# Half tiles, moved normalisations and later expert loads in a language-model tower on one core

## What is computed

```
h = table[ids]                                     # gather
h = h + causal_linear_attention(ln(h))             # 16 heads, elu features, then a scaled layer norm
h = h + ln(h) @ CB.T * (SCB / 127) + bias
h = h + block(ln(h))                               # random-feature attention, norm, relu FF 256-1024-256, norm
x = ln(h)
logits = x @ router_w.T                            # 8 experts, the best one is taken
score  = sigmoid(max(logits));  e = argmax(logits)
moe    = (silu(x*score @ gate[e]) * (x*score @ up[e])) @ down[e]
shared = (silu(x @ sgate) * (x @ sup)) @ sdown
out    = h + moe + shared
```

## Time and profile before

| | us |
|---|---|
| runs, median of three | 697.4 (695.35 to 697.88) |
| the profiled run, its own time | 697.74 |
| its span, first to last instruction | 695.9 |
| dense stage, to the end of the last `send_home` | 541.0 |
| from there to the first expert matmul (547.0) | 6.0 |
| expert matmuls of 23 tiles and the last add | to 692.2 |
| last scatter and its landing | to 695.9 |

### The profile page before, as it was taken

One profiled execution on the slowest core, in us unless ns is written; L12 is line 12 of the kernel. 1 busy time (PEld: TensorE's weight loads), 2 busy tenths in 40 slices (PEclk: granted clock), 3 DMA queues, 4 the chain that ended last, 5 costly groups with the idle time before them and its releaser, 6 DMA issues.

```text
span 695.9 us, 15601 instructions
## 1 busy us (share of the span) xinstructions
PE 638.5 (92%) x5962; PEld 518.7 (75%) x5963; DVE 496.9 (71%) x1156; ACT 288.8 (41%) x696; POOL 256.4 (37%) x414
## 2 busy tenths in 40 slices
PE   5887799998999999999999999999938699999996
PEld 4666687886888888888888989989937365655654
DVE  3988999999999989899989988886515122223231
ACT  2345456546565454546545445553310122222121
POOL 5342335435335152332504323312200355454442
PEclk9998999999999999999999999999987899999999
DMA  7950000000000000000000000003372211011110
GB/s 262 414 223 1 9 9 10 1 17 9 9 17 2 24 2 16 2 16 15 5 16 2 16 17 3 17 16 108 26 186 67 79 40 55 28 42 61 58 52 13
DMA packets 17299, 34.22 MB, mean 49 GB/s; under 512 B 7617, under 2 KB 12240, under 8 KB 15952
## 3 DMA queue, kind: packets, MB, share of 16 engines
q1 hardware_dynamic: 11776, 18.59, 7.4%
q0 software_dynamic: 4592, 8.41, 4.1%
q10 hardware_dynamic: 864, 6.29, 3.9%
HBM read 28.74 MB, written 7.29 MB: 52 GB/s over the span
## 4 chain that ended last, share of the span: by engine, by line
PE 68%; DVE 17%; issue 6%; DMA 4%; ACT 3%; another core or an unknown queue 0%; SPq 0%; POOLq 0%; POOL 0%; DVEq 0%; ACTq 0%
PE ps L1086 63%; DMA home_rows<-send_home 3%; PE ps L1091 2%; DVE stats L710 2%; DVE S_sb L769 2%; DVE rdenTA L792 1%; PE ps L1246 1%; DVE H L726 1%; DVE rdenTB L903 1%; ACT qkA L686 1%; DVE qf L882 1%; DVE mv L711 1%; DMA yA<-x_rows,ids 1%; ACT yTB L676 1%; DVE qkA L755 1%
## 5 line engine op out<-in xcount | busy, mean ns | idle before, releaser
L1086 PE MATMUL ps<-yTC,we 128*128 128x128 f32 x1024 | 124.9, 278 | 0.0
L1086 PEld LDWEIGHTS ps<-yTC,we 128*128 128x128 f32 x1024 | 121.5, 195 | 1.2 <-issue 0.2
L368 POOL TENSOR_TENSOR var_eps<-mv,ln_eps 128x1 f32<-128x1 f32 x112 | 24.3, 217 | 256.8 <-DVE mv L711 255.0
L1086 PE MATMUL ps<-we,yTA 128*128 128x256 f32 (+1 forms) x288 | 97.9, 476 | 3.2 <-DVE S_sb L769 1.4
L1086 PEld LDWEIGHTS ps<-we,yTA 128*128 128x128 f32 x288 | 55.4, 201 | 27.5 <-issue 22.3
L1086 PE MATMUL ps<-we,yTB 128*128 128x256 f32 (+1 forms) x216 | 72.8, 468 | 0.0
L369 POOL TENSOR_TENSOR rstd<-var_eps,pow_half 128x1 f32<-128x1 f32 x112 | 65.6, 586 | 8.8
L1086 PE MATMUL ps<-we,ffT 128*128 128x256 f32 x256 | 60.8, 380 | 0.0
L1086 PEld LDWEIGHTS ps<-we,yTB 128*128 128x128 f32 x216 | 39.7, 190 | 23.4 <-issue 21.0
L1086 PEld LDWEIGHTS ps<-we,ffT 128*128 128x128 f32 x256 | 47.2, 190 | 7.4
L578 ACT ACTIVATE kf<-kf 128x1024 f32<-128x1024 f32 x16 | 16.9, 1059 | 73.4 <-DVE kf L891 73.4
(11 more groups left out here) (189 smaller groups left out, 1364.5 us busy)
## 6 DMA issues: line engine op xcount, KB each, us to landing
we<-w_experts SPq DMA_DIRECT2D x4, 1536.0 KB
we<-w_experts ACTq DMA_DIRECT2D x3, 1536.0 KB
we<-w_ff SPq DMA_DIRECT2D x2, 1024.0 KB
x_rows<-send_x SPq DMA_DIRECT2D x16, 128.0 KB, 1.7
home_rows<-send_home SPq DMA_DIRECT2D x16, 128.0 KB, 1.8
rows_sb<-rows SPq DMA_DIRECT2D x1, 1664.0 KB, 6.4
we<-w_experts ACTq DMA_DIRECT2D x3, 512.0 KB, 3.9
we<-w_qk SPq DMA_DIRECT2D x2, 512.0 KB
```

Of the source, the lines that this page charges most:

```text
L368: link(pool.tensor_tensor(var_eps[:, k:k + 1], mv[:, k, 1:2], ln_eps[:], ALU.add))
L1086: return pe.matmul(o, a, b, start=start, stop=stop)
```

## The change

1. **Normalisations.** Norms 0, 2, 3 and 6 leave VectorE. GpSimd makes rstd as before and then two more products: mean * rstd, and that times -1 (`centre_at`). ScalarE then writes `Identity(x * rstd + centre)`.
2. **Tiles.** The expert stage has 10 rounds of two tiles: 16 whole tiles (W) and 4 tiles (H) that are each two halves of 64 tokens, each half with an expert of its own. An expert's rest of up to 64 tokens takes a half. A half's weights are fetched into `half_w`, which lies over h and the scores buffer (`H_S`), by a register-addressed DMA of 1.5 MB: two for each H tile. TensorE runs a half as a matmul with 64 stationary columns into 64 output partitions, the two halves by turns. New tables (`half_tables`, 22 small VectorE instructions) follow the last step.
3. **Loads.** Experts 4 to 7 are loaded by SP, after the first gather was transposed, instead of by ScalarE in the dense stage's last units. TensorE waits per tile for a count of experts (`experts_ready`), which SP raises.
4. **Order.** PSUM banks are dealt out anew, the four lists of steps are written in another order, waits that go with shared banks are others, and the expert loops are unrolled.

The core of the diff:

```diff
-    SORTED_TILES = T + E - 1
+    WHOLE, HALVES = T, E
+    SHAPES = ["WW", "WW", "WW", "WH", "WW", "WH", "WW", "WH", "WW", "WH"]
-    IDS_FROM = [0, MOE_SLOTS, 2 * MOE_SLOTS, 6 * MOE_SLOTS, SORTED_TILES]
+    IDS_FROM = [0, MOE_SLOTS, 2 * MOE_SLOTS, 3 * MOE_SLOTS, 5 * MOE_SLOTS, 7 * MOE_SLOTS, TILES]
...
             def ids3(t):
                 if t == T - 1:
+                    sp.wait_ge(S["table_ready"], 3)
                     load_ids(3)
             run_steps([
-                (0, x_out), (8, ids2), (2, ids0), (5, ids1), (3, home_out), (8, ids3),
+                (3, home_out), (1, ids0), (6, ids1), (8, ids2), (0, x_out), (8, ids3),
             ])
+            for name, count in (("ffn0_psum", T), ("out1_psum", T), ("ff2_psum", 2 * T), ("gate_psum", T), ("up_psum", T),
+                                ("down_psum", T), ("xT_psum", MOE_SLOTS)):
+                sp.wait_ge(S[name], count)
+            load_late(RESIDENT)
+            load_late(RESIDENT + 1)
+            load_ids(4)
+            load_late(RESIDENT + 2)
+            load_late(RESIDENT + 3)
+            sp.wait_ge(S["tile_done"], T)
+            sp.wait_ge(S["table_ready"], 2)
+            load_halves(0)
+            load_ids(5)
+            sp.wait_ge(S["residents_loaded"], 16 * RESIDENT)
+            sp.sem_inc(S["experts_ready"], 1)
+            for e in range(RESIDENT, E):
+                sp.wait_ge(late_loaded[e], 16)
+                sp.sem_inc(S["experts_ready"], 1)
+            for m in range(1, HALVES // 2):
+                before_it = [j for j in range(TILES) if KIND[j] == "H"][m - 1]
+                sp.wait_ge(S["ey_psum"], before_it + 1)
+                load_halves(m)
...
+            def deviation_and_centre(k, t):
+                link(inverse_deviation(k, t))
+                link(pool.tensor_tensor(centre_at[:, k:k + 1], mv[:, k, 0:1], rstd[:, k:k + 1], ALU.mult))
+                pool.tensor_tensor(centre_at[:, k:k + 1], centre_at[:, k:k + 1], minus_one[:], ALU.mult
+                                   ).then_inc(S[f"centre{k}_ready"], 1)
...
-            def normalise(dst, src, k, t):
-                dve.wait_ge(S[f"rstd{k}_ready"], t + 1)
-                return dve.tensor_scalar(dst, src, mv[:, k, 0:1], rstd[:, k:k + 1], ALU.subtract, ALU.mult)
+            def normalise(dst, src, k, t):
+                act.wait_ge(S[f"centre{k}_ready"], t + 1)
+                return act.activation(dst, src, ACT.Identity, bias=centre_at[:, k:k + 1], scale=rstd[:, k:k + 1])
...
+            def by_halves(o, x, at, n, chunks):
+                for c in range(chunks):
+                    for h in range(2):
+                        ins = matmul(o[h * HALF:(h + 1) * HALF], x[:, c, h * HALF:(h + 1) * HALF],
+                                     half_w[h][:, at + c * n:at + c * n + n], c == 0, c == chunks - 1)
+                return ins
...
+                for s, j in tiles_of(i):
                     pe.wait_ge(S["xT_ready"], j + 1)
+                    if KIND[j] == "W":
+                        pe.wait_ge(S["experts_ready"], need[s] if i < ALL_BY else E - RESIDENT + 1)
```

More of the change, by code:

```diff
@@ L47, in bass_lm_tower @@
     EXPERT = w_experts.shape[2]
-    SORTED_TILES = T + E - 1
-    ROUNDS = -(-SORTED_TILES // MOE_SLOTS)
+    HALF = P // 2
+    WHOLE, HALVES = T, E
+    SHAPES = ["WW", "WW", "WW", "WH", "WW", "WH", "WW", "WH", "WW", "WH"]
+    ROUNDS = len(SHAPES)
+    TILES = MOE_SLOTS * ROUNDS
+    KIND = "".join(SHAPES)
+    NUMBER = [KIND[:j].count(KIND[j]) for j in range(TILES)]
     SPAN = T + 1
@@ L65, in bass_lm_tower @@
         we = sb("we", [P, E * EXPERT])
-        H = sb("H", [P, T, D])
+        H_S = sb("H_S", [P, 2 * EXPERT])
+        H = H_S[:, 0:T * D].rearrange("p (t d) -> p t d", t=T)
+        S_sb = H_S[:, T * D:2 * EXPERT].rearrange("p (b a n) -> p b a n", b=4, a=4)
+        half_w = [H_S[:, h * EXPERT:(h + 1) * EXPERT] for h in range(2)]
         send_x, send_home = sb("send_x", [P, D]), sb("send_home", [P, D])
         nowhere = sb("nowhere", [P, E * SPAN + 1], U32)
-        ids = sb("ids", [P, SORTED_TILES], U32)
+        ids = sb("ids", [P, TILES], U32)
         idx_sb = sb("idx_sb", [P, T], U32)
@@ L110, in bass_lm_tower @@
         full = columns(T)
-        number = columns(SORTED_TILES)
+        number = columns(T + E - 1)
         start_row = columns(E)
@@ L209, in bass_lm_tower @@
         gathered = [sem(f"gathered{t}") for t in range(GATHERS)]
+        late_loaded = {e: sem(f"late_loaded{e}") for e in range(RESIDENT, E)}
+        half_loaded = [sem(f"half_loaded{h}") for h in range(2)]
         x_loaded = [sem(f"x_loaded{s}") for s in range(MOE_SLOTS)]
@@ L257, in tiles_of @@
         def tiles_of(i):
-            of_round = [(s, i * MOE_SLOTS + s) for s in range(MOE_SLOTS)]
-            return [(s, j) for s, j in of_round if j < SORTED_TILES] if isinstance(i, int) else of_round
+            return [(s, i * MOE_SLOTS + s) for s in range(MOE_SLOTS)]
         block = ctx.enter_context(nc.Block())
@@ L475, in ids_for @@
             def ids_for(i):
-                for n in range(4):
+                for n in range(GROUPS):
                     if IDS_FROM[n] == i * MOE_SLOTS:
-                        pool.wait_ge(S[f"ids_loaded{n}"], 16 * (IDS_FROM[n + 1] - IDS_FROM[n]))
+                        pool.wait_ge(S[f"ids_loaded{n}"], 16 * sum(2 if kind == "H" else 1 for kind in KIND[IDS_FROM[n]:IDS_FROM[n + 1]]))
             pool.drain()
@@ L626, in c_th @@
                 act.activation(tC[:], ga, ACT.Tanh, scale=0.5).then_inc(S["tanh_gate"], 1)
-            def load_experts(first, last, done):
-                for e in range(first, last):
-                    act.dma_start(we[:, e * EXPERT:(e + 1) * EXPERT], w_experts[e]).then_inc(S[done], 16)
-            def free_b(t):
-                if t == T - 1:
-                    act.wait_ge(S["ffn0_psum"], T)
-                    act.wait_ge(S["out1_psum"], T)
-                    load_experts(RESIDENT, freed_by_b, "experts_loaded")
@@ L688, in _ @@
             read_xT(0)
-            with act.Fori(0, ROUNDS - 2) as i:
-                expert_tiles(i, [i + 1])
-            expert_tiles(ROUNDS - 2, [ROUNDS - 1])
-            expert_tiles(ROUNDS - 1, [])
+            for i in range(ROUNDS):
+                expert_tiles(i)
         @block.vector
@@ L1000, in table1 @@
                     return
-                link(dve.tensor_tensor(first_tile, ends, need, ALU.subtract))
+                link(dve.tensor_tensor(first_tile, ends, pairs, ALU.subtract))
                 link(dve.scalar_tensor_tensor(out=shift, in0=first_tile, scalar=float(-P), in1=start_row,
@@ L1076, in expert_tiles @@
                                       ).then_inc(S["ey_ready"], 1)
-            with dve.Fori(0, ROUNDS - 1) as i:
+            for i in range(ROUNDS):
                 expert_tiles(i)
-            expert_tiles(ROUNDS - 1)
         @block.tensor
@@ L1373, in expert_tiles @@
+            def expert_tiles(i):
+                expert, need = {}, {}
+                for s, j in tiles_of(i):
+                    if KIND[j] == "W":
+                        n = NUMBER[j]
+                        expert[s] = pe.value_load(tile_expert[0:1, n:n + 1], min_val=0, max_val=E - 1)
+                        if i < ALL_BY:
+                            need[s] = pe.value_load(tile_need[0:1, n:n + 1], min_val=1, max_val=E - RESIDENT + 1)
                 for s, j in tiles_of(i):
                     pe.wait_ge(S["xT_ready"], j + 1)
-                    for b, at, done in ((1, GATE, "eg_psum"), (2, UP, "eu_psum")):
-                        for c in range(KD):
-                            ins = matmul(banks_of[s][b], xT[s][:, c, :],
-                                         we[:, bass.ds(expert[s] * EXPERT + (at + c * F), F)], c == 0, c == KD - 1)
-                        ins.then_inc(S[done], 1)
```

300 lines of the change are left out of this document (170 added, 130 removed).

## The result

| | before | after |
|---|---|---|
| runs, median | 696.9 us (6 runs, 695.35 to 697.88) | 690.8 us (6 runs, 687.9 to 693.1) |
| ratio | | 0.9916 [0.9892, 0.994] |
| a second measurement | 697.0 | 691.8; ratio 0.9898 [0.9862, 0.9934] |
| the profiled run, its own time | 697.74 | 689.3 |
| its span | 695.9 | 687.5 |

A forecast was written before the change was run, and what follows sets the result against it. TensorE bounds full dense units, shares the bound with VectorE from 60 to 200 us; tile count and start time bound the expert stage. -15.5 - 18.1 + 25.0 - 5 = -13.6: span 682.3, median 684, range 668 to 698.

The forecast's parts named there:

- the stall: Dense stage's end: TensorE's 12.8 us of idling and the lower clock behind it go, -15.5 us together.
- norms and order: Dense stage: VectorE freed of 32 us of norm work, paying only where VectorE binds; -5 us.
- the wait for SP: Expert stage's start: first matmul 31 us behind the last `send_home`, waiting for SP's list; +25.0 us.
- the rounds: Expert stage: fewer rounds, first expert matmul to last add 127.1 us instead of 145.2; -18.1 us.
- nothing keeps the small copies: Dense stage's end: with no expert loads before the first gather, the 12.8 us of idling go.
- What is late next there is TensorE itself: Behind the removed stall TensorE sets the pace, its work there the same in both kernels; part of -15.5.
- half of 9.6: 60 to 200 us: 9.6 of VectorE's freed 32 us fall there, about half shows; a gain of 5 taken.
- the large issues: SP's list behind the last `send_home`: issuing four late expert loads and two halves, 4.2 us, at most 9.8.
- the tables' 5.1: Behind the last `send_home`: VectorE's 22 linked `half_tables` instructions take 5.1 us of the wait.
- The 32-column rows: Profile rows: four side-by-side 32-column matmuls cost 1.11 of one whole; used to price four H tiles at 1.0 us.
- The conditions named: Profile signs expected afterwards, plus refutations: expert start within 20 us, H rounds over 14, last `send_home` after 525.5.
- the case's own: The main forecast's own range, 671 to 694 us, given a chance of 0.74.

The follow-up runs named there:

- its second profile: The changed kernel measured once more, unchanged: 691.8 us, 0.9898; the profiled run's span 6.4 us longer than in the first profile.
- the whole list taken away: Changed kernel with SP raising `experts_ready` for experts 0 to 3 ahead of the dense stage's copies: 665.8 us, 0.9549.
- eight of its loads: Changed kernel with SP raising `experts_ready` ahead of its last group of eight token-number loads: 681.2 us, 0.976.
- moving two lines: Changed kernel with SP's wait and `experts_ready` count for experts 0 to 3 moved ahead of the dense stage's copies: 665.8 us, 0.9549.
- the late halves: Changed kernel with SP asking for the second to fourth pair of halves 8.9 us later by plan: 707.7 us, one run.
- both repairs and the early registers: Changed kernel with early `experts_ready` count, GpSimd's scatter four steps later, and TensorE's first-round registers read before the first transposes: 659.5 us, 0.9457; again 659.7.

## Why the prediction came out too low

Of the 5.2 us inside the span, 2.1 belong to the stall, 0.8 to norms and order, 0.9 to the wait for SP, 0.9 to the rounds and 0.5 to the tail behind the last add, which was taken as unchanged. Every term erred to the same side.

*The stall.* Its cause was right: loads put back bring it back. Its worth was 13.4 us, not 15.5: from the 12th `send_home` to the last, 37.5 us became 24.1. The step that failed is "nothing keeps the small copies" and, with it, "What is late next there is TensorE itself": any further wait for the copies was put at nothing. Next was the same copy again. The median of 1.8 us had been taken for a property of the copy; it was one of the order of the queues. Before, `x_rows` and `home_rows` were issued some 6.5 us ahead of the scatter of that unit; the change writes GpSimd's and SP's lists anew, and now the scatter goes out, in most units, 2.5 to 3 us ahead of the copies. In two units of the changed kernel it goes out 4 and 6.5 us ahead, and these copies are through soonest, 3.9 and 3.7 us after their issue. The trace records each copy's landing in 16 parts. The scatter issued at 496.8 us lands from 500.3 to 504.4. The copy of `home_rows` issued at 499.3 has all its data out by 501.1, but half of its landings come at 503.8 to 503.9 and the other half at 507.2 to 507.3, and those of `x_rows` at 507.2 to 507.5, just as those of the next scatter (issued at 501.8) begin, at 507.4. The Trainium skill (DMA: Bandwidth & Descriptors, Queues, rings and completion order) says that a semaphore increment lands only after every earlier write of the same DMA engine, also those of its other queues. That fits the first half of the landings; the second half came 2.8 us after the earlier scatter had landed, so more than the rule is at work there, and what it is stays open. That the scatter is the cause is shown by moving it: 1.5 to 3.7 us of the drain went, and the landings in full units are back at 1.7. The drain then takes 22.1 to 22.6 us, and the forecast, 37.5 less 15.5, had 22.0: without the scatter ahead of the copies no more than 0.1 to 0.6 of this term's miss is left. The order of GpSimd's list against SP's was there to read in the change; the prediction looked at SP's list only behind the dense stage.

*Norms and order.* At the 12th `send_home` the changed kernel is 4.2 us ahead (503.1 to 498.9), for 5 forecast; in its second profile, with the later start, it is not ahead at all (503.4). That 4.2 is near 5 is luck. The prediction took 32 us off VectorE; up to the 12th `send_home` its busy time fell by 21.2 (441.0 to 419.8), since other instructions of it became longer (`mark` with `cols_sb` from 0.17 to 0.49 us each in full units, the sum x from 0.47 to 0.71), for a reason that no run shows. And 29 us of work put back on VectorE cost 9 us, so VectorE's time was worth 0.3 of itself, in full units too, where the prediction had nothing: it took half of 9.6. What the longer chain of a norm takes back was set at 2; the two numbers, 9 and 4.2 or less, leave 5 or more. Whether that is the chain or the new order was not settled: the norms themselves were not moved back in any run.

*The wait for SP.* Right in mechanism and size: 32.3 us from the start of `send_home`, 31.9 from its end, where 31.0 were forecast. Three kernels confirm it: the whole list taken away gives 26 us, eight of its loads 10, and the data were ready. Its terms erred both ways: 4.2 for the large issues was 3.2 by itself, and the gaps between SP's groups (waits, register reads of the halves) took 3.2 more; the tables' 5.1 did not show, since nine loads run on from 524.5 us without a break; the token-number loads were 24.0 us for 22, cheaper than 1.19 each.

*Rounds.* 128.0 us for 127.1, which looks better than it is: the H tiles cost 3.3 in place of 1.0, the second term that was mis-sized, and the whole rounds hid 1.4 of it, being 0.11 shorter each than before (12.23 for 12.34, with whole tiles only). Why they are shorter was not looked into. The 32-column rows gave the right price for streams side by side and the wrong one for the borders: four packed groups in a long packed stretch have few of them. The Trainium skill (TensorEngine Tiling (Array Packing), Key Properties) has a change of the tiling mode drain the engine; the estimate made from it was 4.4 us in place of 1.0. The 3.3 of the runs lie nearer to that rule than to the row: about 0.14 us at each of an H round's four changes, half of the 278 ns of one matmul, and 0.9 once that this rule does not explain. That the time between the matmuls is such a drain, no run shows. The prediction weighed the rule and chose the row; that cost 2.3.

*The conditions named.* No wait for `home_rows` before the last units, as stated; the one of 3.3 us falls in the drain, and the text did not look there. First expert matmul within 29 to 37 us: yes. Idle time under 8 us from 60 to 200: 4.9. H rounds within 0.6 us of the others: 0.65, and 1.6 for the first. Last `send_home` before 525.5: 523.4, so the bound was too wide to catch a miss of 2.9.

*The rest.* 1.5 us are the profiled run's distance to the median. By the second profile, which is 6.4 us longer, such a distance lies almost wholly in the dense stage: there its gain over the kernel before is 11.3 us, not 17.6. The range of 668 to 698 held the time, and so did the case's own, 671 to 694.

## What to carry to other kernels

A semaphore that one engine counts up at the end of a long list prices that whole list for whoever waits: here 1.1 us for each register-addressed load, 26 us in all, and moving two lines gave four times what the change gave. When queues are reordered, the landing time of a small copy is not a constant: look at what writes, also from other queues, are issued just ahead of it. Idle time marked "issue" ahead of a group often is register reads that can stand where the engine waits anyway.

## What the runs showed of the hardware

**A short stand of TensorE costs more than itself.** After the 5 us waits for the late halves TensorE's next group took 5.35 to 6.50 us in place of 3.65. The waits sum to 15 us, the rounds lost 22. The granted clock behind the first wait was 0.50 (1.2 GHz) from 625 to 629 us and back at 1.00 from 631; in the changed kernel it is 1.00 through the same matmuls.

**Two profiles of one kernel differ at the start, and the difference stays.** The kernel with both repairs and the early registers was profiled twice, with spans of 654.7 and 661.1 us. Its stretches 5:10, 10:15, 15:20 and 20:25 us in the first profile:

```profile
5.00:10.00 5.00, 3.29 (x40) 3.12 (x38) 0.74 (x3) 0.60 (x1) 3.29 (x9) 1.00 0.86 298
10.00:15.00 5.00, 4.43 (x22) 3.91 (x21) 0.47 (x2) 1.07 (x4) 2.42 (x6) 0.66 1.00 360
15.00:20.00 5.00, 2.62 (x27) 1.95 (x27) 2.30 (x5) 2.75 (x7) 0.00 (x0) 1.00 1.03 370
20.00:25.00 5.00, 4.10 (x64) 2.98 (x62) 3.76 (x9) 2.70 (x8) 2.32 (x6) 1.00 1.01 399
```

and in the second:

```profile
5.00:10.00 5.00, 2.82 (x38) 2.65 (x36) 0.61 (x3) 0.60 (x1) 3.17 (x9) 0.98 0.86 297
10.00:15.00 5.00, 4.43 (x19) 4.06 (x20) 0.61 (x2) 0.39 (x2) 2.56 (x6) 0.50 1.00 358
15.00:20.00 5.00, 3.46 (x24) 2.02 (x24) 1.61 (x4) 3.43 (x9) 0.00 (x0) 0.84 1.05 370
20.00:25.00 5.00, 5.00 (x50) 4.56 (x53) 3.39 (x7) 1.69 (x6) 1.79 (x5) 0.66 1.00 399
```

The granted clock (the third number from the end) is at its lower level of 1.2 GHz through parts of the first 25 us, in one of the four stretches of the first profile and in all four of the second. The ninth yTA copy comes at 75.8 and at 80.3 us; these 4.5 us are the larger part of the 6.4 between the two spans. The lower clock and the late copies go together; which makes the other was not tried. Over thirteen profiles of the changed kernel and its variants this copy comes between 74.3 and 80.3. The kernel before, at 75.9, held 2.4 GHz through its first 30 us in its one profile, but its runs, too, reached from 691.8 to 699.9 beside the last experiments, so it is not shown that the longer first norm makes the start worse. Sixteen more matmuls ahead of it did not keep the clock up. What would is open.
